# Tiles of 512 instead of 448 pixels, three images in hand, no loop, and other SBUF addresses in a two-layer expert convolution

## The reference

```python
xn = group_norm(x)                                   # 32 groups, no scale
top_v, top_i = top_k(softmax(xn @ gate_w + gate_b), 2)
top_w = softmax(top_v)
coef[e] = sum_k present[k, e] * top_w[k]             # present: expert e is a k-th choice anywhere
h[e] = relu(w1[e] @ xn + b1[e])                      # 384 x 384
out = x + sum_e coef[e] * (w2[e] @ h[e] + b2[e])     # 384 x 384
```

## Time and profile before

| | |
|---|---|
| median of 3 runs | 2561.24 us (2560.88 to 2562.74) |
| the profiled execution, its own time | 2562.41 us |
| its span, first to last instruction | 2560.6 us |
| PE, DVE, ACT, POOL busy | 2524.1, 1453.8, 487.3, 74.3 us |
| matmuls / instructions | 12,890 / 33,748 |
| HBM read, written | 146.03, 41.75 MB |

### The profile page before, as it was taken

How to read it: one execution, slowest core, us unless ns; L and a number is a source line. 1 busy time by engine, 2 the same in 40 slices (tenths; PEclk the granted TensorE clock), 3 DMA queues, 4 the chain that set the end, 5 groups by cost and what they waited for, 6 DMA issues and landing times.

```text
span 2560.6 us, 33748 instructions
## 1 busy us (share of the span) xinstructions
PE 2524.1 (99%) x12890; PEld 2297.9 (90%) x12890; DVE 1453.8 (57%) x3130; ACT 487.3 (19%) x845; POOL 74.3 (3%) x44
## 2 busy tenths in 40 slices
PE   5999999999999999999999999999999999999999
PEld 4899999999999999999999999999999999999998
DVE  7665564655656555556646556565655555565543
ACT  3211211111111121111112111111111211121111
POOL 3000000000000000000000000000000000000000
PEclk8999999999999999999999999999999999999999
DMA  4332213323123221132220322312322223231120
GB/s 161 89 84 76 60 53 88 100 61 81 51 68 100 76 85 57 46 100 79 82 76 26 98 80 80 79 33 90 96 65 78 66 56 100 60 89 52 45 76 22
DMA packets 193432, 190.07 MB, mean 74 GB/s; under 512 B 29808, under 2 KB 191856, under 8 KB 193264
## 3 DMA queue, kind: packets, MB, share of 16 engines
q1 hardware_dynamic: 193264, 187.81, 26.0%
HBM read 146.03 MB, written 41.75 MB: 73 GB/s over the span
## 4 chain that ended last, share of the span: by engine, by line
PE 96%; DVE 2%; DMA 1%; issue 1%; POOL 0%; ACT 0%; SPq 0%; DVEq 0%; POOLq 0%; ACTq 0%
PE z_ps L422 16%; PE z_ps L423 16%; PE z_ps L424 16%; PE y_ps L442 16%; PE y_ps L443 16%; PE y_ps L441 16%; PE g_ps L309 1%; DMA rows<-rows_dram 0%; DVE x_raw L290 0%; DMA x_raw<-in_x 0%; DVE h_lo L481 0%; DVE x_lo L302 0%; POOL w_lo L768 0%; POOL rstd L279 0%; DMA rows_dram<-wrow 0%
## 5 line engine op out<-in xcount | busy, mean ns | idle before, releaser
L470 DVE SCALAR_TENSOR_TENSOR hid<-z_ps,b_sb,rows 128x448 f32<-128x448 f32 x668 | 454.3, 680 | 898.8 <-PE z_ps L424 885.5
L441 PE MATMUL y_ps<-h_lo,w_hi 128*128 128x448 f32 x2016 | 737.5, 366 | 10.7 <-DVE h_lo L481 10.4
L424 PE MATMUL z_ps<-x_hi,w_hi 128*128 128x448 f32 x2016 | 741.6, 368 | 0.0
L423 PE MATMUL z_ps<-x_hi,w_lo 128*128 128x448 f32 x2016 | 741.4, 368 | 0.0
L422 PE MATMUL z_ps<-x_lo,w_hi 128*128 128x448 f32 x2016 | 740.5, 367 | 0.6 <-DVE x_lo L302 0.6
L442 PE MATMUL y_ps<-h_hi,w_lo 128*128 128x448 f32 x2016 | 737.9, 366 | 0.0
L443 PE MATMUL y_ps<-h_hi,w_hi 128*128 128x448 f32 x2016 | 737.7, 366 | 0.0
L477 ACT ACTIVATE h_hi<-hid 128x448 fp32r<-128x448 f32 x672 | 385.7, 578 | 1690.2 <-DVE hid L470 1676.9
L481 DVE SCALAR_TENSOR_TENSOR h_lo<-hid,h_hi 128x448 fp32r<-128x448 f32 x672 | 414.3, 616 | 25.1 <-ACT h_hi L477 24.8
L422 PEld LDWEIGHTS z_ps<-x_lo,w_hi 128*128 128x128 f32 x2016 | 379.7, 188 | 45.1 <-issue 10.9
L441 PEld LDWEIGHTS y_ps<-h_lo,w_hi 128*128 128x128 f32 x2016 | 378.5, 188 | 45.5 <-DVE h_lo L481 10.3
(11 more groups left out here) (86 smaller groups left out, 369.5 us busy)
## 6 DMA issues: line engine op xcount, KB each, us to landing
rows<-rows_dram SPq DMA_DIRECT2D x78, 560.0 KB, 7.3
x_raw<-in_x SPq DMA_DIRECT2D x62, 588.0 KB, 7.7
res<-in_x SPq DMA_DIRECT2D x80, 336.0 KB, 3.7
out<-res SPq DMA_DIRECT2D x78, 336.0 KB, 3.2
rows<-rows_dram SPq DMA_DIRECT2D x16, 840.0 KB, 7.1
res<-in_x SPq DMA_DIRECT2D x16, 504.0 KB, 6.0
out<-res SPq DMA_DIRECT2D x16, 504.0 KB, 5.8
rows<-rows_dram SPq DMA_DIRECT2D x16, 280.0 KB, 6.8
```

What stands on the lines that cost most here:

```text
L423: nc.tensor.matmul(z, w1_lo[:, e, j, ks], hi, start=False, stop=False)
L424: ins = nc.tensor.matmul(z, w1_hi[:, e, j, ks], hi, start=False, stop=(j == NJ - 1))
L441: nc.tensor.matmul(y, w2_hi[:, e, k, ms], h_lo[:, slot], start=first, stop=False)
L470: nc.vector.scalar_tensor_tensor(hid[:, q % HIDS], z_ps[:, q % ZB, 0:T], b1_sb[:, e, k:k + 1], coef, ALU.add, ALU.mult).then_inc(scaled, 1)
```

## The change

The tile has 512 pixels, the whole of a PSUM bank, and runs over all images: 25,088 pixels are 49 tiles, without groups. x_hi and x_lo hold two tiles (not a ring of images), so a tile's operand is always one run; the split of x into them is made per tile, in one or two pieces by image, in chunks 2 to 4 of the tile before. x_raw has three slots instead of two; an image's load stands about 32 chunks before its first tile. The coefficient rows of all images have their own place in DRAM, and a tile's rows come in one DMA. All engines' programs are written out without a loop. At the start, image 1 is loaded right behind the weights, and its statistics and its first piece of x_lo come before the first `scale`, its normalisation after chunks 0 and 1. x_hi, x_lo, h_hi and h_lo, the moving operands of the products, are allocated first, at the lowest addresses, and the weights behind them. The arithmetic is the same.

```diff
-IMAGES = 4
-GROUPS = B // IMAGES
-T = 448
-TILES = IMAGES * PIX // T
-SLOTS = 2
+T = 512
+TILES = B * PIX // T
+SLOTS = 3
...
+        x_hi = sb("x_hi", [P, 2, NJ, T], f32r)
+        x_lo = sb("x_lo", [P, 2, NJ, T], f32r)
+        h_hi = sb("h_hi", [P, RING, T], f32r)
+        h_lo = sb("h_lo", [P, RING, T], f32r)
         w1_hi = sb("w1_hi", [P, E, NJ, HID], f32r)
...
         x_raw = sb("x_raw", [P, SLOTS, NJ, PIX])
-        x_hi = sb("x_hi", [P, NJ, SLOTS * PIX], f32r)
-        x_lo = sb("x_lo", [P, NJ, SLOTS * PIX], f32r)
...
+        def split_x_hi(act, t, i):
+            b, lo, n, at = pieces(t)[i]
+            act.wait_ge(main.xn_ready, HALVES * b + (2 if lo + n > HALF else 1))
+            if t >= 2:
+                act.wait_ge(z_ready, TILE_CHUNKS * (t - 1))
+            nc.scalar.copy(x_hi[:, t % 2, :, at:at + n], x_raw[:, b % SLOTS, :, lo:lo + n]).then_inc(
+                main.xhi_ready, 1)
...
-                    hi, lo = moving(x_hi, j, t), moving(x_lo, j, t)
+                    hi, lo = x_hi[:, t % 2, j], x_lo[:, t % 2, j]
...
+        def place_of(sp, n):
+
+            before = n - SLOTS
+            sp.wait_ge(main.xlo_ready, parts_to(last_tile(before) - 1) + 1)
+            sp.wait_ge(main.gate_ready, before + 1)
...
+        def preparing(q):
+
+            for n in range(2, B):
+                off = q - (TILE_CHUNKS * first_tile(n) - LEAD)
+                if -8 <= off <= 15:
+                    yield n, off
...
+            stats(dve, main, 1, 1, 0, lk)
+            stats(dve, main, 1, 1, 1, lk)
+            group_stats(dve, main, 1, lk)
+            split_x_lo(dve, 1, 0)
             dve.wait_ge(wlo_ready, 2 * E - 1)
-            scale(dve, Group(0, 0, 0, first=True), 0)
+            scale(dve, 0)
+            for q in range(CHUNKS):
+                t, r = divmod(q, TILE_CHUNKS)
...
                 if q == 0:
-                    stats(dve, main, 1, 1, 0, lk)
-                    stats(dve, main, 1, 1, 1, lk)
-                    group_stats(dve, main, 1, lk)
-                if q == 1:
                     norm_columns(dve, main, 1, lk)
                     normalise(dve, main, 1, 1, 0)
+                if q == 1:
+                    normalise(dve, main, 1, 1, 1)
                 if q == 2:
-                    normalise(dve, main, 1, 1, 1)
+                    split_x_lo(dve, 1, 1)
...
+                for i in range(2):
+                    if r == 2 + i and t and t < TILES - 1 and i < PIECES[t + 1]:
+                        split_x_lo(dve, t + 1, i)
...
+            for h in range(HALVES):
+                load_x(sp, main, 1, 1, h)
             sp.wait_ge(flag_ready, 1)
...
+            for q in range(CHUNKS):
+                t, r = divmod(q, TILE_CHUNKS)
...
+                if r == 2 and t and t < TILES - 1:
+                    rows_in(sp, t + 1)
+                if r == 4 and t:
+                    store(sp, t - 1)
+                if r == 5 and t and t < TILES - 1:
+                    load_res(sp, t + 1)
+                for n, off in preparing(q):
+                    if off == -6 and n > 2:
+                        place_of(sp, n)
+                        for h in range(HALVES):
+                            load_x(sp, main, n, n % SLOTS, h)
+                    if off == 13:
+                        rows_out(sp, n)
...
+            for u in range(UNITS):
+                if u == 1:
+                    gate_product(pe, main, 1, 1)
+                for n in range(2, B):
+                    if NK * u == TILE_CHUNKS * first_tile(n) - LEAD + 8:
+                        gate_product(pe, main, n, n % SLOTS)
+                if 0 < u < UNITS - 1:
+                    mm1(pe, u + 1, chunks=range(2 if u == 1 else 0, NK))
+                mm2(pe, u)
```

More of the change, by code:

```diff
@@ L31, with parts_to, slot_parts, first_tile @@
 SCAN_LINKS = 37
[L32 to L37, removed]
-def pieces(t):
[L43 to L51, removed]
+LEAD = 26
+def pieces(t):
+    parts, at = [], T * t
+    while at < T * (t + 1):
+        b, lo = divmod(at, PIX)
+        n = min(PIX - lo, T * (t + 1) - at)
+        parts.append((b, lo, n, at - T * t))
+        at += n
+    return parts
+PIECES = [len(pieces(t)) for t in range(TILES)]
+def parts_to(t):
+    return sum(PIECES[:t + 1])
+def slot_parts(t):
+    return sum(PIECES[t % 2:t + 1:2])
+def first_tile(n):
+    return n * PIX // T
+def last_tile(n):
+    return ((n + 1) * PIX - 1) // T
 def conv_moe(nc, x, gate_w, gate_b, w1, b1, w2, b2, out):
@@ L393, in find_present, with mm1 @@
             lk.link(nc.vector.tensor_scalar(present[:, :], g_ps[:, 0:2 * E], 0.5, None, ALU.is_gt))
[L395 to L406, removed]
+        def mm1(pe, u, chunks=range(NK)):
             t, e = divmod(u, E)
-            if G.first and t == 0:
+            if t == 0:
                 pe.wait_ge(wlo_ready, 1 + e)
             if e == 0:
-                pe.wait_ge(main.xlo_ready, G.g * (HALVES * IMAGES) + t + 2)
+                pe.wait_ge(main.xlo_ready, parts_to(t))
             for k in chunks:
                 q = NK * u + k
-                if G.first and ZB <= q < ZB + EARLY:
+                if ZB <= q < ZB + EARLY:
                     pe.wait_ge(early_done, q - ZB + 1)
-                elif not (G.first and q < ZB):
-                    pe.wait_ge(scaled, G.chunk(q - ZB + 1))
-                z = product(z_ps[:, q % ZB], t)
+                elif q >= ZB:
+                    pe.wait_ge(scaled, q - ZB + 1)
+                z = z_ps[:, q % ZB]
                 ks = slice(k * P, (k + 1) * P)
                 for j in range(NJ):
-                    hi, lo = moving(x_hi, j, t), moving(x_lo, j, t)
+                    hi, lo = x_hi[:, t % 2, j], x_lo[:, t % 2, j]
                     nc.tensor.matmul(z, w1_hi[:, e, j, ks], lo, start=(j == 0), stop=False)
@@ L425, in mm1, with mm2 @@
                 ins.then_inc(z_ready, 1)
-        def mm2(pe, G, u):
+        def mm2(pe, u):
             t, e = divmod(u, E)
-            tail = G.last and u == UNITS - 1
-            if G.first and t == 0:
+            tail = u == UNITS - 1
+            if t == 0:
                 pe.wait_ge(wlo_ready, 1 + E + e)
@@ L522, in each_group @@
-        def each_group(eng, group):
-            group(Group(0, 0, 0, first=True))
-            with eng.Fori(0, (GROUPS - 2) // 2) as i:
-                group(Group(i * 2 + 1, 1, i * TILES))
-                group(Group(i * 2 + 2, 0, i * TILES + TILES))
-            group(Group(GROUPS - 1, 1, (GROUPS - 2) // 2 * TILES, last=True))
-        def preparing(G, q):
-            for k in range(1, IMAGES + 2):
-                off = q - (PERIOD * k - LEAD)
-                if 0 <= off < PERIOD and not (G.last and k >= IMAGES) and not (G.first and k == 1):
-                    yield k, off
@@ L705, in _ @@
                 weight_hi(0, e)
-            for h in range(HALVES):
-                split_x_hi(act, 0, 0, h)
+            split_x_hi(act, 0, 0)
             weight_hi(0, 3)
@@ L780, in _ @@
                     inverse_std(pool, scan, b - 1)
-            with pool.Fori(1, B) as b:
-                inverse_std(pool, main, b)
+            for n in range(1, B):
+                inverse_std(pool, main, n)
         @block.sync
@@ L901, in _ @@
             gate_product(pe, main, 0, 0)
-            start = Group(0, 0, 0, first=True)
-            mm1(pe, start, 0)
+            mm1(pe, 0)
             sum_counts(pe, main)
-            mm1(pe, start, 1)
-            mm1(pe, start, 2, chunks=range(2))
+            mm1(pe, 1)
+            mm1(pe, 2, chunks=range(2))
             pe.wait_ge(flag_ready, 1)
```

378 lines of the change are left out of this document (124 added, 254 removed).

## The result

The changed kernel takes 2485.6 us, median of 4 runs (2484.28 to 2486.27), beside 2562.0 us (2560.88 to 2562.81) for the kernel before on the same chip: a ratio of 0.9702 [0.9689, 0.9714], 76.4 us less. I had forecast 33 less. The direction was right, the size was not: the time lies inside the range, but near its low end and in the ground of rival (b), the falling remainder.

A forecast was written before the change was run, and what follows sets the result against it. TensorE bound it: from 100 us on, time is products times step. Fewer matmuls 26.3 + startup 5.8 + loop edges 0.8 - tail 0.1 = 32.8 us; 2562.4 - 32.8 - 1.2 = 2528 us, range 2475 to 2562.

The forecast's parts named there:

- rival (b): Product step: remainder falls, as operands start at low multiples of 2048 bytes; 2475 us at 12.4 ns, 2344 without remainder; chance 0.13.
- I take r' = r: Product step: the time beyond columns over clock stays 17.4 ns per matmul at 512 columns, a step of 230.7 ns.
- I cost the edit at nothing: SBUF allocation: moving operands low and weights above change only addresses, and the rows show no price for a high address.
- rival (c): Product step: remainder rises to 23.3 ns if all operands lie at the place of the 0.21 us steps; 2591 us, chance 0.10.
- fewer matmuls save their remainder: Tiles of 512: 10,584 products instead of 12,096, so 1512 remainders of 17.4 ns fall away, 26.3 us.
- Rival (a): Product step: remainder grows with the columns to 19.9 ns, so longer tiles save nil; 2555 us, chance 0.14.
- Rival (d): Each tile: a new wait, SP's single file or the x split late by 1 us per tile; 2577 us, chance 0.05.
- Startup: PE's first second-layer products: of 10.4 us of waits for h_lo about 4.6 stay, 5.8 us saved; first scaling 0.8 us later.
- the slack of the early products: Startup: PE's 72 early products end 1.9 us before h_lo comes and grow by 1.9 us, just hidden.
- Startup and loop edges: Outside the steady products: startup saves 5.8 us, two inner loop edges 0.8 us, the tail grows 0.1 us.
- the idle cover for them: VectorE idles 899 us ahead of L470, nearly all for z, which covers its longer steps and the x split's extra 3 us.
- the DMA slack: Loads: rows land in 7.3 us while a tile's products take 49.8 us, so loads asked a tile ahead make no wait.

The follow-up runs named there:

- experiment 1: The changed kernel with the weights first in SBUF again and the moving operands above them: 2563.1 us, ratio 1.0005.
- the two scans: The changed kernel with x operands shifted tile by tile, two tiles per shift, once at 512 columns and once at 448; only mean steps were read, no total time.
- experiment 11: The changed kernel with weights first and 352 unused bytes ahead of x_raw, so moving operands lie high but at distance 0 modulo 256: 2484.8 us, 0.9697.
- experiment 13: The changed kernel with tiles of 448 and all moving operands 64 bytes past the weights modulo 256: 2505.4 us, 0.9778.
- experiment 9: The changed kernel with products using only the first 512 to 256 columns, varied by tile; only mean steps were read, its total time is no result.
- experiment 2: The changed kernel with tiles of 448 instead of 512, moving operands still at the lowest addresses: 2548.5 us.

## Why the prediction was wrong

**Wrong: "I take r' = r", and with it "I cost the edit at nothing" for the addresses.** The remainder of a step isn't one number per matmul. It depends on how far the moving operand lies from the weights, modulo 256 bytes, and on the columns: 13.5 to 23.2 ns at 512, 13.3 to 21.5 at 448 in the two scans. The kernel before stood at 17.4; the change put all operands at distance 0, where 512 columns have 13.45. That term was 26.3 us in the sum and measured 67.8. Nothing in the prediction aimed at distance 0, and with the weights first the same change ends at 1.0005 (experiment 1), so that it came out faster at all is in part luck.

My reason for the nothing was that the lower of two operands had the longer step. That answered the question of low against high, and there it was right (experiment 11: the height does nothing). The question that decides, where the operand lies against the weights, I didn't ask. The single steps in the same rows were a hint that the remainder isn't one number: the trace, which keeps nanoseconds, has 202 to 207. It was no more than a hint, since experiment 13, at the floor, has steps from 197 to 202. The 0.21 us step itself, from which I took 23.3 ns as the upper end and 2591 us for rival (c), was a rounding of the view: the trace has 204 ns for it.

**Right in kind, mis-sized: fewer matmuls save their remainder.** 1512 x 17.4 = 26.3 us was forecast; between good places (13 and the changed kernel) it is 19.8 us, and 1512 x 13.3 is 20.1. Rival (a), the remainder that grows with the columns, is out: at 320 columns it is 13.3 ns (experiment 9), at 512 13.45.

**Rival (b)** had the mechanism's direction and its price per ns: 10.6 us x 3.95 = 42 us below the forecast, as it came. Its cause, multiples of 2048 bytes at low addresses, isn't what the runs show. The rule that I weighed there, of the Trainium skill, "TensorE: Matmul & The Clock Gate", section "Wait — 56ns, not 53.3ns?", would give N/2.4 + 2.5 = 215.8 ns at 512; the runs have 226.8 at best, so they don't bear it out for these operands.

**Rival (c)**, the rise, was real, one allocation away: experiment 1 has 20.95 ns, and I had put the point from which the change is slower at 21.0. It ended at 1.0005. **Rival (d)** didn't show: no wait of PE after 100 us.

**Startup:** of 10.4 us of waits I kept 4.6; it is 2.9. The first `scale` came 3.2 us later, not 0.8, because one short step of the statistics (L254), 0.19 us elsewhere, took 2.63 us. It ended at 48.69, just behind GpSimd's second `w_lo` (45.95 + 2.69 = 48.64), and so it does in the eight other traces where it starts beside that step. In experiment 2 the second `w_lo` ran from 44.08 to 46.74, and there the step before, L253, took 2.45 us and ended at 46.77. So these steps of VectorE stood until GpSimd's was through; I had counted no such wait. VectorE is busy without a break from L254 to the h_lo that ends PE's 2.94 us, so some 2.63 - 0.19 = 2.4 us of that wait hang on it, an estimate; no run moved `w_lo` away. I had also read the slack of the early products wrongly, as 1.9 us where the row gives 1.52 of idle time; with h_lo this late it made no difference. Startup and loop edges gave 8.6 us for 6.5; the waits for h_lo alone fell by 7.5. The lengths of VectorE's steps (747, 681 ns for 747, 683), the idle cover for them, the DMA slack and the instruction fetch (1.78 MB in the two queues for 27,783 instructions, 64 bytes each) came as worked out.

## What to carry to other kernels

Where TensorE's products stand back to back, take the step apart into columns over the clock and a remainder. Then move the moving operands against the weights by a few unused columns and look again, for each tile length anew; whether single steps of one shape are even doesn't tell a good place from a bad one. A change of tile size or of an allocation's order moves that place by accident, so time it with the place held, or its own effect can't be told: here the longer tile, with the rest of the change, was worth nothing at one place (experiment 1), and by itself 20 us between good places (13 against the changed kernel).

## What the runs showed that I had not expected

The mean step of a product in a steady stream depends on the distance of its two operands in SBUF with a period of 256 bytes: at 512 columns 226.9 ns at 0, 236.6 four bytes on, 227.1 at 256, and 226.8 four bytes short of 512. The Trainium skill, "SBUF — State Buffer", section "SBUF: two separate sides", says that among the engines only the port pair of VectorE and GpSimd makes anyone wait. The 2.63 us of L254 beside `w_lo` fit that. But these runs also show a price that hangs on the places of TensorE's own two operands, which that sentence doesn't foresee; whether it is paid at a port no run here shows. What stops it isn't settled. The weights of the next product are loaded while one streams (in the changed kernel's trace the load for the product of 1205.83 starts at 1205.60, with the product ahead of it, and takes 0.19 us), so the two may meet, but no run here changed the load alone. Open too is why the first products behind a switch still carry the step of those ahead, why 13.3 ns stay at the best places, at 320, 448 and 512 columns alike, and why none is seen at half clock.
